# One key chunk of attention in fp16 halves, with the token work moved between blocks

## The reference, cut to what matters

```python
x1 = layernorm(x)                                  # x: [4096, 128]
q, k, v = x1 @ Wq, x1 @ Wk, x1 @ Wv                # 2 heads of 64
scores = where(adj > 0, q k^T / 8, -9e15)          # [2, 4096, 4096]
sat = softmax(scores) @ v
out = concat(sat[:2048] @ weightr, sat[2048:] @ weightd) + bias
x = x + leaky_relu(out, 0.01)
x2 = layernorm(x)
idx = top_k(x2 @ Wg + bg, 2)
x = x + sum over the chosen experts e of gelu(x2 @ W1[e] + b1[e]) @ W2[e] + b2[e]
```

## Time and profile before

| | us |
|---|---|
| median of 3 runs | 838.68 |
| the three runs | 839.06, 837.7, 838.68 |
| the profiled execution | 838.33 |
| its span in the profile | 836.4 |
| PE, ACT, DVE, POOL busy | 801.3, 684.9, 622.3, 252.2 |

### The profile page before, as it was taken

One profiled execution on the slowest core, in us unless ns is written; L12 is line 12 of the kernel. 1 busy time (PEld: TensorE's weight loads), 2 busy tenths in 40 slices (PEclk: granted clock), 3 DMA queues, 4 the chain that ended last, 5 costly groups with the idle time before them and its releaser, 6 DMA issues.

```text
span 836.4 us, 32096 instructions
## 1 busy us (share of the span) xinstructions
PE 801.3 (96%) x12080; PEld 596.4 (71%) x12080; DVE 622.3 (74%) x1469; ACT 684.9 (82%) x1099; POOL 252.2 (30%) x362
## 2 busy tenths in 40 slices
PE   4899999999999999999999999999997799999997
PEld 1367777777777777777777777777776567777775
DVE  6687788887978888887888888788874475555555
ACT  3668888888888888888888887888886789999996
POOL 4021031212203031121303112130210657766674
PEclk9999999999999999999999999999999999999999
DMA  8644333433443344334334433433100000000000
GB/s 222 112 66 69 66 59 63 77 64 56 66 72 56 57 72 72 56 61 77 56 56 64 78 59 56 77 61 56 31 1 2 2 14 15 14 14 13 13 13 13
DMA packets 40902, 44.98 MB, mean 54 GB/s; under 512 B 22168, under 2 KB 32160, under 8 KB 40864
## 3 DMA queue, kind: packets, MB, share of 16 engines
q0 software_dynamic: 9216, 33.56, 25.2%
q1 hardware_dynamic: 31216, 10.71, 5.5%
q10 hardware_dynamic: 432, 0.20, 0.1%
HBM read 71.72 MB, written 2.10 MB: 88 GB/s over the span
## 4 chain that ended last, share of the span: by engine, by line
PE 73%; POOL 14%; issue 8%; DVE 3%; ACT 1%; DMA 1%; POOLq 0%; DVEq 0%
PE ps L960 29%; PE ps L927 20%; PE ps L942 18%; POOL prob L395 14%; PE ps L971 2%; PE ps L885 1%; PE ps L890 1%; PE ps L898 1%; PE ps L979 1%; DMA x_sb<-in_x 1%; DVE prob L640 1%; ACT pt L420 0%; DVE stats L562 0%; POOLq L394 0%; ACT k_half L430 0%
## 5 line engine op out<-in xcount | busy, mean ns | idle before, releaser
L640 DVE CUSTOM_DVE_ANT_0 prob<-ps,mask 128x1024 f32<-128x1024 f32 x256 | 312.2, 1221 | 77.5 <-PE ps L927 65.2
L462 ACT ACTIVATE prob<-prob,nmax 128x1024 f32<-128x1024 f32 x256 | 292.8, 1144 | 0.4 <-DVE nmax L648 0.4
L960 PE MATMUL ps<-pt,v_sb 128*64 128x128 f32 x4096 | 251.9, 276 | 0.0
L960 PEld LDWEIGHTS ps<-pt,v_sb 128*64 128x64 f32 x4096 | 221.0, 137 | 12.6 <-issue 5.0
L942 PEld LDWEIGHTS ps<-ident,prob 64*128 64x128 f32 x4096 | 152.2, 138 | 62.7 <-issue 61.6
L927 PE MATMUL ps<-k_half,q_row 64*128 64x512 f16 x1536 | 188.6, 376 | 1.9 <-DVE k_half L599 1.5
L942 PE MATMUL ps<-ident,prob 64*128 64x64 f32 x4096 | 179.8, 227 | 7.2 <-DVE pt L656 3.7
L302 POOL DMA_DIRECT2D mask<-in_adj x64 | 36.8, 576 | 417.8 <-DVE low L640 417.8
L475 ACT ACTIVATE pt<-ps 128x1024 f32<-128x1024 f32 x128 | 131.0, 1024 | 34.2 <-PE ps L942 33.0
L395 POOL TENSOR_TENSOR prob<-prob 128x512 f16<-128x512 f32 x104 | 122.6, 1183 | 57.2 <-ACT prob L532 54.6
L839 DVE SCALAR_TENSOR_TENSOR x_sb<-ps,k_half,x_sb 128x128 f32 (+1 forms) x256 | 72.2, 344 | 79.0 <-PE ps L1080 78.0
(11 more groups left out here) (105 smaller groups left out, 705.9 us busy)
## 6 DMA issues: line engine op xcount, KB each, us to landing
mask<-in_adj POOLq DMA_DIRECT2D x64, 512.0 KB, 5.6
q_row<-q_nat SPq DMA_DIRECT2D x128, 32.0 KB, 4.8
x_sb<-in_x SPq DMA_DIRECT2D x4, 512.0 KB, 7.0
out<-x_sb SPq DMA_DIRECT2D x8, 256.0 KB, 2.3
x2t_hi<-in_L_ffn_W SPq DMA_DIRECT2D x1, 1024.0 KB, 6.3
wq_sb<-in_L_gnn_Wq ACTq DMA_DIRECT2D x1, 64.0 KB, 2.9
wk_sb<-in_L_gnn_Wk ACTq DMA_DIRECT2D x1, 64.0 KB, 4.5
wv_sb<-in_L_gnn_Wv ACTq DMA_DIRECT2D x1, 64.0 KB, 5.8
```

Source lines behind the costliest of these rows:

```text
L462: act.activation(prob[:, h, cols], prob[:, h, cols], ACT.Exp, bias=nmax[:, h:h + 1], scale=-1.0, accum_out=sums[:, j, h, p:p + 1]).then_in ...
L640: dve.tensor_tensor_reduce(out=prob[:, h, col_of(p)], in0=ps[:, 2 * (u % 2):2 * (u % 2) + 2, :].rearrange("p b c -> p (b c)"), in1=mask[:, ...
L960: ins = pe.matmul(ps[dims, AV, 0:P], v_sb[:, tile, dims], pt[:, UNITS.index((h, p)), t, :], start=(tile == 0), stop=(tile == NT - 1))
```

## The change

Key chunk 1 of every tile (units 1 and 3, `SPLIT_P`, `SPLIT_UNITS`) is multiplied in fp16. ACT and DVE copy its transposed probabilities to `pt_raw`. POOL makes a high half in fp16 with a one-input instruction and a low half by subtraction, and PE multiplies high by high, high by low and low by high, 48 matmuls for 32 instructions of fp32. The value rows of the chunk are split once at the start; Wv is scaled up by 32 before and the output weights down by 32. The other chunks stay fp32.

POOL's step starts with the two splits; between them it waits until DVE has made the first half of the next mask. The residual moves from odd to even steps. DVE's `make_mask` moves from after units 3 and 7 to after units 2 and 4, `finish_tile` from u = 2 to u = 4. `AV_BLOCK` becomes 2: each chunk of values is multiplied one block later, chunk 1 in block 3. The token work changes places: on DVE `divide` to u = 6 of odd steps, `leaky` to u = 0 and `statistics` to u = 6 of even steps, `x2t_low` to u = 2 and `keep_logits` to u = 4 of odd steps; on PE `out_project` to block 2, `x2_transpose` and `logits` to blocks 0 and 1 of the next odd step; on ACT `x2t_high` to u = 2 of odd steps.

```diff
-AV_BLOCK = 1
+AV_BLOCK = 2
+SPLIT_P = 1
+SPLIT_UNITS = (1, 3)
+WHOLE = (0, 2, 4, 5, 6, 7)
+V_UP = 2.0 ** 5
...
+            def split_values():
+
+                raw = v_sb[:, SPLIT_P * KT:(SPLIT_P + 1) * KT, :]
+                pool.wait_ge(v_ready, 2 * SPLIT_P + 2)
+                pool.tensor_scalar(v_pair[:, 0, :, :], raw, 1.0, 0.0, ALU.mult, ALU.add).then_inc(v_hi_ready, 1)
+                pool.wait_ge(v_hi_ready, 1)
+                pool.tensor_tensor(v_pair[:, 1, :, :], raw, v_pair[:, 0, :, :], ALU.subtract).then_inc(v_lo_ready, 1)
+
+            def split_pt(j, u, early=False):
+
+                q = u // 2
+                pool.wait_ge(pt_by_act, NU * j + u + 1)
+                pool.wait_ge(pt_by_dve, copies_by_dve(j, u + 1))
+                if not early:
+                    pool.wait_ge(av_done, NP * j + SPLIT_P - 3)
+                pool.nop(nofuse=True)
+                pool.tensor_scalar(pt_hi[:, q, :, :], pt_raw[:, q, :, :], 1.0, 0.0, ALU.mult,
+                                   ALU.add).then_inc(pt_hi_by_pool, 1)
+                pool.wait_ge(pt_hi_by_pool, 2 * j + q + 1)
+                pool.tensor_tensor(pt_lo[:, q, :, :], pt_raw[:, q, :, :], pt_hi[:, q, :, :],
+                                   ALU.subtract).then_inc(pt_by_pool, 1)
...
-            def step(i, par, post=True, load=True, split=True):
-
+            def step(i, par, prior=True, post=True, ahead=True, load=True, split=True, early=False):
+
+                if prior:
+                    split_pt(i - 1, 1, early)
+                    if ahead:
+                        pool.wait_ge(mask_ready, 2 * i + 3)
+                    split_pt(i - 1, 3, early)
+                if load:
+                    load_adj(i + 2, par, 0)
+                if post and par == 0:
+                    residual(i - 4)
+                if split and par == 0:
+                    split_ffn_part(i)
                 if post and par == 0:
                     inverse_std(i - 4)
                     normalise(i - 4)
                 if load:
-                    load_adj(i + 2, par, 0)
-                if split and par == 0:
-                    split_ffn_part(i)
-                if load:
                     load_adj(i + 2, par, 1)
-                if post and par == 1:
-                    residual(i - 3)
...
-                    if post and u == 6:
-                        x2t_high(i - 4)
+                    if post and u == 2:
+                        x2t_high(i - 5)
...
-                    if finish and u == 2:
+                    if finish and u == 4:
                         finish_tile(i - 2, par)
...
-                    if ahead and u in (3, 7):
+                    if ahead and u in (2, 4):
                         make_mask(i + 1, 1 - par, u // 4)
                     if post and par == 1:
-                        if u == 0 and ready:
-                            keep_logits(i - 5)
                         if u == 0:
                             invert_sums(i - 3)
-                        if u == 4:
+                        if u == 2 and ready:
+                            x2t_low(i - 5)
+                        if u == 4 and ready:
+                            keep_logits(i - 5)
+                        if u == 6:
                             divide(i - 3)
-                        if u == 6:
-                            leaky(i - 3)
                     if post and par == 0:
                         if u == 0:
+                            leaky(i - 4)
+                        if u == 6:
                             statistics(i - 4)
-                        if u == 6:
-                            x2t_low(i - 4)
...
+                    if p == SPLIT_P:
+                        for values, probs in ((0, pt_hi), (0, pt_lo), (1, pt_hi)):
+                            for h in range(HEADS):
+                                dims = slice(h * DH, (h + 1) * DH)
+                                ins = pe.matmul(ps[dims, AV, 0:P], v_pair[:, values, t, dims], probs[:, h, t, :],
+                                                start=False, stop=False)
...
-                    if post and par == 1 and k == 1:
-                        out_project(i - 3)
...
-                    if post and par == 0 and k == 2:
-                        x2_transpose(i - 4)
-                    if post and par == 0 and k == 3:
-                        logits(i - 4)
+                    if post and par == 1 and k == 0 and ready:
+                        x2_transpose(i - 5)
+                    if post and par == 1 and k == 1 and ready:
+                        logits(i - 5)
+                    if post and par == 1 and k == 2:
+                        out_project(i - 3)
```

More of the change, by code:

```diff
@@ L180, in build @@
         pt_by_dve = sem("pt_by_dve")
+        pt_hi_by_pool = sem("pt_hi_by_pool")
+        pt_by_pool = sem("pt_by_pool")
+        wv_scaled = sem("wv_scaled")
+        v_hi_ready = sem("v_hi_ready")
+        v_lo_ready = sem("v_lo_ready")
         av_done = sem("av_done")
@@ L371, in _ @@
                     load_adj(i, i, c)
-            step(0, 0, post=False, split=False)
+            step(0, 0, prior=False, post=False, split=False)
+            split_values()
             pool.wait_ge(w1_in, 16)
@@ L379, in _ @@
             pool.tensor_scalar(ident16[:, :], ident[:, :], 1.0, 0.0, ALU.mult, ALU.add).then_inc(w_split_chain, 1)
-            step(1, 1, post=False)
+            pool.tensor_scalar(wrd[:, :, :, :], wrd[:, :, :, :], 1.0 / V_UP, 0.0, ALU.mult, ALU.add).then_inc(w_split_chain, 1)
+            step(1, 1, post=False, early=True)
             step(2, 0, post=False)
@@ L384, in _ @@
             step(NT - 2, 0, load=False)
-            step(NT - 1, 1, load=False)
-            step(NT, 0, load=False, split=False)
+            step(NT - 1, 1, load=False, ahead=False)
+            step(NT, 0, load=False, ahead=False, split=False)
             inverse_std(NT - PAIR)
@@ L468, in copy_pt @@
                 act.wait_ge(transposed, NU * j + u + 1)
-                if not early:
-                    act.wait_ge(av_done, NP * j + p - 3)
+                if u in SPLIT_UNITS:
+                    if not early:
+                        act.wait_ge(pt_by_pool, 2 * j + u // 2 - 1)
+                    to = pt_raw[:, u // 2, :, :]
+                else:
+                    if not early:
+                        act.wait_ge(av_done, NP * j + p - 3)
+                    to = pt[:, WHOLE.index(u), :, :]
                 if u in DVE_COPIES:
-                    act.activation(pt[:, u, :, 0:DH], ps[:, TR0, :].rearrange("p (k q) -> p k q", k=KT),
+                    act.activation(to[:, :, 0:DH], ps[:, TR0, :].rearrange("p (k q) -> p k q", k=KT),
                                    ACT.Copy).then_inc(pt_by_act, 1)
                 else:
-                    act.activation(pt[:, u, :, :].rearrange("p k (b q) -> p b k q", b=2),
+                    act.activation(to.rearrange("p k (b q) -> p b k q", b=2),
                                    ps[:, TR0:TR0 + 2, :].rearrange("p b (k q) -> p b k q", k=KT),
@@ L507, in _ @@
             step(3)
[L508 to L511, removed]
+            step(4)
+            step(5, post=True)
+            pairs(act, 6, NT, lambda i, par: step(i, post=par == 1))
+            step(NT, now=False, last=True)
+            x2t_high(NT - 2 * PAIR)
             act.wait_ge(b1_in, 16)
@@ L653, in copy_pt @@
                 dve.wait_ge(transposed, NU * j + u + 1)
-                if not early:
-                    dve.wait_ge(av_done, NP * j + p - 3)
-                dve.tensor_copy(pt[:, u, :, DH:P],
+                if u in SPLIT_UNITS:
+                    if not early:
+                        dve.wait_ge(pt_by_pool, 2 * j + u // 2 - 1)
+                    to = pt_raw[:, u // 2, :, :]
+                else:
+                    if not early:
+                        dve.wait_ge(av_done, NP * j + p - 3)
+                    to = pt[:, WHOLE.index(u), :, :]
+                dve.tensor_copy(to[:, :, DH:P],
                                 ps[:, TR0 + 1, :].rearrange("p (k q) -> p k q", k=KT)).then_inc(pt_by_dve, 1)
@@ L798, in _ @@
             choose_gates(0, 0, RANKED_EARLY)
+            x2t_low(NT - 2 * PAIR)
             keep_logits(NT - 2 * PAIR)
@@ L948, in attend @@
                 ready = BOTH_HEADS[p] + 1
-                pe.wait_ge(pt_by_act, NU * j + ready)
-                pe.wait_ge(pt_by_dve, copies_by_dve(j, ready))
+                if p == SPLIT_P:
+                    pe.wait_ge(pt_by_pool, 2 * j + 2)
+                else:
+                    pe.wait_ge(pt_by_act, NU * j + ready)
+                    pe.wait_ge(pt_by_dve, copies_by_dve(j, ready))
                 if p == 0 and not first:
@@ L955, in attend @@
                 pe.nop(nofuse=True)
+                if p == SPLIT_P and first:
+                    pe.wait_ge(v_lo_ready, 1)
                 for t in range(KT):
                     tile = p * KT + t
[L958 to L961, removed]
```

(23 more changed lines are left out.)

14 lines of the change are left out of this document (11 added, 3 removed).

## The result

The changed kernel takes 852.8 us (median of four, 852.76 to 853.26) against 838.9 (837.7 to 843.2) for the kernel before on the same chip: a ratio of 1.017, 95% interval 1.015 to 1.019, so 14 us slower. The forecast was 851.0, range 843 to 860. The profiled execution of the changed kernel took 852.82 with a span of 851.1; that of before 838.33 with 836.4. The span grew by 14.7 us.

What follows compares the result with a forecast made beforehand. PE bounds the kernel (96% busy), but VectorE's in-order queue would eat the gain: odd steps +10.3, even +0.3, slower first transposes +2.0, steps 1 and 2 -0.9, start +0.6, together +12.3, so 851.0 us, range 843 to 860.

Steps and rivals of the forecast that it cites:

- The fp16 chunk: Key chunk 1 on PE: 48 fp16 matmuls in 1.43 us instead of 1.90, 0.47 us a step if nothing else were late.
- The rival of 2.7 us: Key chunk 1 on PE: the two heads don't overlap in fp16, chunk takes 2.7 us, total 864; chance 0.05.
- The odd step's end: divide before copy 7 delays transposes(0) to 3.81 us after score unit 6, before 3.12; PE waits 1.15, +0.69 us.
- No second wait: After copy 7: copy 0 follows by 1.93 us, transposes(1) can go at 2.88, PE comes at 2.96, so no wait.
- The even step's end: statistics before copy 7: transposes(0) 3.15 us after score unit 6, before 3.36; with logits paid in odd steps, +0.02 us.
- The gain lost in the wait: End of odd steps: the chunk's whole 0.47 us is lost while PE waits for VectorE's in-order queue.
- Mask preparations and GpSimd: Preparations at u = 2 and 4 and two GpSimd splits a step (3.1 us each, at most 4.9) cost nothing; cover thin.
- the rival: GpSimd's split holds up the mask preparation: 0 to 35 us on top, 855 with a 3.8 us split; chance 0.15.
- The test named in the prediction: On VectorE: if mask preparations last longer than 0.69 us, the rival of GpSimd's splits holding them up holds.
- The start: Step 0: two mask preparations, not one, come before the row maximum that ACT's first exponential waits for; +0.60 us.
- The tail: Last step, copy 0 to the FFN's first matmul: 20.9 us before, 20.8 in the new order; 0, between -2 and +2.

Runs made afterwards that it cites:

- e4_quad: Changed kernel with VectorE's loop of two steps written as a loop of four, same instructions and order: 849.2 us, 1.013 of the kernel before.
- e1_fp32: Changed kernel with key chunk 1 kept in fp32 and no GpSimd splits, every move kept: 854.65 us, 1.020 of the kernel before.
- e5_leaky: e3_both with the leaky step one unit later, in score unit 2 of the even step: 832.15 us, 0.991 of the kernel before.
- e7_leaky_fp32: e5_leaky with key chunk 1 in fp32 and no GpSimd splits: 841.65 us, 1.002 of the kernel before.
- e2_divide: Changed kernel with divide and leaky both after mask unit 1 of the even step: 854.1 us, 1.018 of the kernel before.
- e3_both: e2_divide with statistics also moved one unit earlier, from u = 6 to u = 5: 848.5 us, 1.011 of the kernel before.
- e6_both_fp32: e3_both with key chunk 1 in fp32 and no GpSimd splits: 837.9 us, 0.998 of the kernel before.
- e8_leaky_quad: e5_leaky with VectorE's loop of two steps written as a loop of four: 830.8 us, 0.990 of the kernel before.

## Why the prediction was right, step by step

**The fp16 chunk: right.** 1.43 us was taken, between bounds of 1.34 and 2.7. The chain after has, early in the run where nothing waits behind it:

```profile
69.71 1.46 PE ps L1027 x48
71.17 0.64 PE ps L1002 x16
```

48 matmuls in 1.46 us, 0.030 each: the heads overlap. The rival of 2.7 us is dead.

**The odd step's end: right in kind, too large.** From the end of score unit 6 to transposes(0) the prediction had 3.81 us; it is 409.48 - 406.08 = 3.40, before 3.12. Two terms were too big. The division was taken at 1.57 us, from its first instruction to the next mask, but copy 7 does not wait for its results, and enters 408.64 - 407.36 = 1.28 us behind its start: 0.3 of the 1.57 belonged to the mask that followed it there. And copy to transposes was taken at 0.95; here it is 409.48 - 408.64 = 0.84. So +0.28 in place of +0.69. TensorE stood idle for 0.73 us there, not 1.15.

**"No second wait": wrong.** It costs 2.49 us between the two groups of transposes instead of 1.94, +0.55 with the slower first group in it. The step that failed is the count "0.60 + 1.15 + 0.18" from copy 7 to copy 0. It had the instructions and no time for the loop's jump, and the sentence that the mask preparation "has been moved away" took as a relief what was the cover of the jump. The idle time can be read nowhere in before, because there it was covered. e4_quad shows it: half the jumps, half the waits, 3.6 us. The two errors on the odd step almost cancel: 0.28 + 0.55 = 0.83, forecast 0.69 + 0.07. That is luck.

**The even step's end: right in kind, again too large.** The same stretch is 427.54 - 424.64 = 2.90, forecast 3.15, before 3.36, with 0.23 us of TensorE idle, not 0.5. The statistics hold VectorE for 426.70 - 425.92 = 0.78, not 0.91, and copy to transposes is 0.84 here too. With the logits' 0.24 paid elsewhere the change is -0.22, forecast +0.02.

**Left out: the second group of transposes.** The prediction made only the first group behind a wait slower. The group after it is slower too, 0.68 us against 0.49 behind an even step and 0.72 against 0.64 behind an odd one: +0.27 a pair. The chain of after, then of before:

```profile
427.54 0.72 PE ps L1002 x16
428.25 1.29 PE ps L987 x12
429.55 0.68 PE ps L1002 x16
```

```profile
421.64 0.49 PE ps L942 x16
```

A pair as a whole grew by 0.98 (forecast 0.69 + 0.02 + 0.14 = 0.85). Measured it is 0.28 + 0.55 on the odd side, -0.22 + 0.07 on the even side and 0.27 for the second groups, 0.95 in all. Two waits were forecast too long by 0.4 and 0.24, and the jump and the second groups, 0.5 and 0.27, were not in the sum. The loop's +11.9 us (forecast 11.7) is so near because these cancel: the mechanism was right, the closeness is luck.

**The gain lost in the wait: shown.** e1_fp32 has the same period without the chunk, and e5_leaky against e7_leaky_fp32 has the gain back when VectorE is in time.

**Mask preparations and GpSimd.** The split was taken at 3.1 us; it was 1.06 for the one-input form, not 0.83, and 2.14 for the subtraction (a group of the page: count, busy us, mean ns, idle time before). The upper bound of 4.9 is 4.7 by its own terms, 2.4 + 2.3; neither number matters.

```profile
L337 POOL TENSOR_TENSOR pt_lo<-pt_raw,pt_hi 128x1024 f16<-128x1024 f32 x64 | 137.2, 2144 | 5.3
```

The prediction's test for the rival was that preparations last longer than 0.69. They do, and with them VectorE's busy time rose, which it was forecast not to do: the 64 preparations took 55.9 us instead of 43.9. By line, after and then e1_fp32 without splits (ns min, median, max):

```profile
L657 DVE TENSOR_SCALAR mask<-mask x58: 687/818/1011, 78.1 to 610.2; 128x2048 bf16<-128x2048 bf16 x58
```

```profile
L649 DVE TENSOR_SCALAR mask<-mask x58: 687/690/887, 78.5 to 610.5; 128x2048 bf16<-128x2048 bf16 x58
```

So the rival's mechanism is real, and its price in the loop of this kernel is nothing: 41 of these 58 preparations are held up, most for 0.1 to 0.3 us, the tail end of a subtraction, and TensorE does not wait behind them. (In e1_fp32 14 of 58 still last some 0.15 us longer, once a pair; beside what was not looked into.) In step 1 one preparation even took 2.50 us, beside a whole subtraction, and TensorE had no wait behind that one either. The test named in the prediction was too weak for its own rival; the wait behind it is what counts. The prediction gave the cover as thin, 0.29 us, and that is what e2 and e3 ran into when 2.28 us fell on the same spot.

The Trainium skill (SBUF — State Buffer, Who interferes with whom) gives both cases as one rule: a VectorE instruction with two inputs in SBUF, or in a two-port mode, and a GpSimd instruction that reads SBUF have the shared ports one after the other, each for its whole length. The traces agree in size: reckoned from 0.15 us before GpSimd's recorded end and with their own lengths added, the leaky step should end at 416.31 - 0.15 + 0.42 = 416.58 in e2_divide (416.59 in the trace), and the preparation in e5_leaky at 403.76 - 0.15 + 0.69 = 404.30 (404.31). The 0.15 is fitted to the first of these. It holds for the 2.50 us of step 1 as well (65.00 - 0.15 + 0.69 = 65.54, trace 65.55), and for a step of the gate ranking with two inputs in SBUF, 0.39 us by itself, in e4_quad (638.47 - 0.15 + 0.39 = 638.71, trace 638.72):

```profile
636.40 2.32 DVE L801 TENSOR_TENSOR k_half<-logit,k_half 128x224 f32<-128x224 f32 x1
```

```profile
636.32 2.15 POOL L337 TENSOR_TENSOR pt_lo<-pt_raw,pt_hi 128x1024 f16<-128x1024 f32 x1
```

**The start: +1.6, forecast +0.6.** The second mask preparation ahead of the row maximum costs 0.4 to 0.5: so much later than before step 1 begins in e5_leaky and e4_quad (49.62 and 49.69 against 49.21). The other 1.1 to 1.2 is not the change. The first key projections run at half speed in some executions: after, e1_fp32, e3_both and e6_both_fp32 have them at 1.06 us (e2_divide and e7_leaky_fp32 only the first pair), e4_quad, e5_leaky and e8_leaky_quad at 0.59 as before had. After, then e5_leaky, in TensorE's timeline:

```profile
18.93 1.06 PE L948 MATMUL ps<-pt,wk_sb 128*64 128x512 f32 x1
```

```profile
18.89 0.59 PE L948 MATMUL ps<-pt,wk_sb 128*64 128x512 f32 x1
```

The granted clock is recorded as 1.00 in both. What makes the difference was not found.

**The tail: +1.5, forecast 0 (-2 to +2).** Two things stand out. A key chunk of 32 matmuls took 3.36 us instead of 1.90, and the gate ranking stood beside GpSimd's last splits:

```profile
638.69 3.36 PE ps L1032 x32
```

```profile
640.17 1.22 DVE L801 TENSOR_TENSOR k_half<-logit,k_half 128x224 f32<-128x224 f32 x1
```

(the chain of waits, and VectorE's timeline: this ranking step takes 0.39 us in before.) The granted clock of TensorE from 637 to 643 us was 0.72 on average, between its two levels; from 630 to 637 us it was 1.00, with TensorE busy for 5.76 of the 7 us. The other traces tell the two apart. By the starts in the timelines it is 21.6 us before and 22.9 after from the first transposes of step 32 to the FFN's first matmul. e4_quad, whose code is the same there, has its chunk at 1.90, a granted clock of 1.00, and 23.0: in this kernel the slow chunk costs nothing. e1_fp32, without splits, has 21.8. So the +1.5 is nearly all the ranking held up by the splits, though no run moved one of the two alone. In e2_divide, e5_leaky and e8_leaky_quad the slow chunk (3.4 to 3.6 us) stands one place later, and there the same stretch is 25.6, 25.5 and 24.6 against 23.0 in e3_both, which has none. In e5_leaky the granted clock was 0.50 there, its lower level of 1.2 GHz (626 to 632 us). That is 1.6 to 2.6 us of these profiled executions and may be absent in others of the same kernel.

## What to carry to other kernels

When the bound engine waits for an in-order queue at one place, shortening the bound engine's work there is worth nothing: find the queue's length behind the last thing it needs, move side work to where it has slack, and only then is the shorter work seen (here nothing in the period before, 5.75 to 9.5 us of the whole after, by the fp32 order that it is held against). In moving side work to or from VectorE, look at what GpSimd does in the same microseconds: an instruction of 0.42 us grew to 2.28 because it began 0.13 us into a GpSimd subtraction, and one unit later it was harmless. An instruction between two that matter may be hiding a loop jump; before taking it away, reckon the jump in.

## What the runs showed of the hardware that was not expected

- VectorE's loop jump leaves it idle for 0.47 us between two instructions that wait for nothing (12 times, 5.4 us), and for none of it where an instruction of 0.68 us stands in front.
- A VectorE step with two SBUF inputs (0.42 us) took 2.28 us beside a GpSimd subtraction over 1024 columns (2.14 us), while VectorE's copies and mask steps that read PSUM kept their lengths (658 to 693 ns for all copies of the changed kernel, 1205 to 1226 for all its mask steps) whether GpSimd ran or not. GpSimd's subtraction itself never grew: 2131 to 2150 ns in e5_leaky. A GpSimd one-input split that began 0.08 us after a ranking step of VectorE with two SBUF inputs did: 1.22 us in place of 1.05 (after, 639.94).
- fp16 matmuls with 64 columns of weights and 128 moving columns, the two heads in different halves, come at 0.030 us each: 1.46 us for 48, against 1.90 for 32 in fp32.
- The first key projections ran at 1.06 or 0.59 us an instruction in different executions, at the same recorded clock of 1.00.
- After a wait for a copy not only the next 16 transposes are slower (0.72 us for 0.65) but the group behind the scores too (0.68 for 0.49). Why was not tested.
